# Input convolution as a projection, a copy and diagonal taps; split and softplus pieces placed elsewhere

## What is computed

```python
xz = einsum('btm,im->bti', x, W_in); x_d, z = split(xz, 2)      # 256 -> 2 x 512
xc = pad(x_d, 3 in front); xc = depthwise_conv(xc, conv_w)      # 4 taps along the tokens
x_d = silu(xc + conv_b)
dt, B, C = x_d @ W_x.T                                          # 1 + 16 + 16 columns
delta = softplus(dt * W_dt + b_dt)
for each token: h = exp(delta*A)*h + delta*B*x_d;  y = sum_s h*C      # 16 states
y = (y + D*x_d) * silu(z);  out = y @ W_out.T
```

## Time and profile before

| | us |
|---|---|
| median of 3 runs | 1176.44 |
| lowest, highest | 1171.94, 1177.12 |
| the profiled execution, its time | 1170.4 |
| its span, first to last instruction | 1168.6 |
| mixer, start of the gate of tile 0 to that of tile 9 | 99.15 to 742.48 |
| busy over the span: PE, DVE | 995.2 (85%), 958.2 (82%) |
| busy over the span: POOL, ACT | 792.6 (68%), 671.4 (57%) |

### The profile page before, as it was taken

How to read it: one execution, slowest core, us unless ns; L and a number is a source line. 1 busy time by engine, 2 the same in 40 slices (tenths; PEclk the granted TensorE clock), 3 DMA queues, 4 the chain that set the end, 5 groups by cost and what they waited for, 6 DMA issues and landing times.

```text
span 1168.6 us, 16964 instructions
## 1 busy us (share of the span) xinstructions
PE 995.2 (85%) x4739; PEld 757.7 (65%) x4739; DVE 958.2 (82%) x1813; ACT 671.4 (57%) x1780; POOL 792.6 (68%) x840
## 2 busy tenths in 40 slices
PE   6798889888798988989879797667599999999991
PEld 5686666666566665766656675334388888888780
...
GB/s 181 215 326 326 91 23 23 60 14 57 33 35 68 14 60 33 48 50 18 80 10 51 25 23 53 14 61 410 185 186 172 226 274 270 258 264 283 256 258 109
DMA packets 104475, 150.28 MB, mean 129 GB/s; under 512 B 13983, under 2 KB 91231, under 8 KB 103999
## 3 DMA queue, kind: packets, MB, share of 16 engines
...
HBM read 72.32 MB, written 76.82 MB: 128 GB/s over the span
## 4 chain that ended last, share of the span: by engine, by line
PE 47%; DVE 22%; issue 15%; ACT 8%; POOL 3%; DMA 3%; SPq 1%; DVEq 0%; POOLq 0%; ACTq 0%
PE BC L982 11%; PE Y L826 10%; DVE arena L1368 10%; PE F L747 5%; PE Y L976 3%; PE K L844 3%; PE K L996 3%; PE F L996 3%; DMA mixer_own<-pool_dram 2%; DVE arena L1380 2%; PE F L733 2%; PE D L988 1%; ACT arena L1038 1%; PE BC L808 1%; PE K L789 1%
## 5 line engine op out<-in xcount | busy, mean ns | idle before, releaser
L1368 DVE TENSOR_TENSOR_SCAN arena<-D,arena 128x444 f32<-128x444 f32 (+1 forms) x352 | 351.1, 1037 | 12.6 <-ACT D L1087 10.4
L826 PE MATMUL Y<-arena,ident 128*128 128x444 f32 (+1 forms) x704 | 308.4, 566 | 1.6 <-DVE arena L1380 1.6
L684 POOL DMA_INDIRECT gat<-y_dram,slot_all x176 | 175.6, 998 | 126.0 <-issue 105.5
L629 POOL TENSOR_TENSOR arena<-mixer_own,arena 128x888 f32<-128x888 f32 (+1 forms) x90 | 164.9, 1833 | 69.4 <-ACT arena L1075 64.8
L617 POOL DMA_INDIRECT pool_dram<-hrow,slot_of x176 | 175.7, 998 | 45.9 <-issue 38.6
L1087 ACT ACTIVATE D<-mixer_own,aneg 128x216 f32<-128x216 f32 (+1 forms) x384 | 148.2, 427 | 94.5 <-DVE arena L1368 91.8
L629 POOL TENSOR_TENSOR arena<-arena 128x888 f32<-128x888 f32 x75 | 143.6, 1915 | 69.1 <-ACT arena L1075 67.3
L1380 DVE TENSOR_TENSOR arena<-arena,BC 128x888 f32<-128x888 f32 (+1 forms) x176 | 184.9, 1050 | 5.7
L982 PE MATMUL BC<-arena,xt 128*128 x716 | 186.1, 383 | 0.0
L826 PEld LDWEIGHTS Y<-arena,ident 128*128 128x128 f32 x704 | 129.3, 203 | 75.2 <-issue 70.1
L1087 ACT ACTIVATE D<-arena,aneg 128x216 f32<-128x216 f32 x320 | 127.0, 437 | 83.0 <-DVE arena L1368 83.0
...
## 6 DMA issues: line engine op xcount, KB each, us to landing
mixer_own<-pool_dram SPq DMA_DIRECT2D x179, 144.0 KB, 3.7
y_dram<-mixer_own SPq DMA_DIRECT2D x179, 128.0 KB
...
```

Source lines behind the costliest of these rows:

```text
L629: nc.gpsimd.tensor_tensor(cut(drive[g % DRIVES], i), cut(du[i % 2], i), b_row[pooled(g) % B_ROWS][:, None, 0:width(i)].broadcast_to([P, KI ...
L684: nc.gpsimd.indirect_dma_start(out=gat[0:r, k, b, :], out_offset=None, in_=y_rows[0:(blocks_by(t) - k) * P, :], in_offset=bass.IndirectOff ...
L826: mm = nc.tensor.matmul(Y[j][:, 0:w], ident[:], read[g % 3][:, j * w:(j + 1) * w], start=(s == 0), stop=(s == STATES - 1), skip_group_chec ...
L1368: nc.vector.tensor_tensor_scan(state[g % 2][:, lo:hi], D[b][:, 0:hi - lo], drive[g % DRIVES][:, lo:hi], 0.0, ALU.mult, ALU.add).then_inc(s ...
```

## The change

The convolution is no longer folded into the weights. PE projects x (`project_x`: 2 groups x 2 matmuls, with the plain W_in), ACT copies the two groups to SBUF (`copy_x_d`, 128 x 444), and PE applies the 4 taps as 4 matmuls with diagonal 128 x 128 matrices (`diag_w`), and the bias as before. `project_x(n, 1)` stands in PE's step 4, c=2 and c=3 in steps 7 and 8, nothing of it in steps 5 and 6; `project_x` of the tile after next stands in step 14. The copies are in ACT's steps 4 and 14. DVE builds the 16 diagonals at the start instead of the 8 products of `inw4`, and the taps are loaded as 128 x 16 values in place of 128 copies of 2048.

Beside it: DVE's second split piece moves ahead of `reads` in step 12, `softplus_small` from step 12 to ahead of `reads` in step 13; POOL's `multiply_series` moves from step 13 to 14 and waits for `softplus_large`; ACT runs its split pieces ahead of the exp, the router's weights after the gate's tanh, copies B of state 15 early in step 12, and puts the logarithm before the series.

```diff
--- before.py
+++ after.py
@@ pool @@
             def multiply_series(n):
                 pool.wait_ge(series_done, n + 1)
+                pool.wait_ge(soft_sum, n + 1)
...
-                    if i + 1 < TILES and s == 13:
+                    if i + 1 < TILES and s == 14:
                         multiply_series(i + 1)
@@ pe @@
+            def project_x(n, b):
...
+                for c in range(2):
+                    for k in range(KM):
+                        at = 2 * b + c
+                        mm = nc.tensor.matmul(F[:, c * w:(c + 1) * w].rearrange("p (a t) -> p a t", t=TOKENS), inw_x[:, k, at * P:(at + 1) * P],
+                                              h0[n % 3][:, k, 0:images(n), :], start=(k == 0), stop=(k == KM - 1))
+                mm.then_inc(x_d_done, 1)
...
+            def convolve(n, c):
+
+                if c % 2 == 0:
+                    pe.wait_ge(x_d_copied, 2 * n + c // 2 + 1)
...
                 for back in range(TAPS):
-                    nc.tensor.matmul(to.rearrange("p (a t) -> p a t", t=TOKENS)[:, :, back:], inw4[:, k, TAPS - 1 - back, c * P:(c + 1) * P],
-                                     h0[n % 3][:, k, 0:images(n), 0:TOKENS - back], start=(k == 0 and back == 0), stop=False,
-                                     skip_group_check=True)
...
+                    nc.tensor.matmul(to.rearrange("p (a t) -> p a t", t=TOKENS)[:, :, back:], diag_w[:, c, TAPS - 1 - back, :],
+                                     of[:, :, 0:TOKENS - back], start=(back == 0), stop=False, skip_group_check=True)
...
-                if front and s in (4, 5):
-                    convolve(n, 2, s - 4)
+                if front and s == 4:
+                    project_x(n, 1)
...
-                if front and s in (6, 8):
-                    convolve(n, 3, (s - 6) // 2)
+                if front and s in (7, 8):
+                    convolve(n, s - 5)
...
-                    if s in (14, 15):
-                        convolve(i + 2, 0, s - 14)
+                    if s == 14:
+                        project_x(i + 2, 0)
+                    if s == 15:
+                        convolve(i + 2, 0)
@@ act @@
+            def copy_x_d(n, b):
+                act.wait_ge(x_d_done, 2 * n + b + 1)
+                if 2 * n + b > 0:
+                    act.wait_ge(conv_done, KI * n + 2 * b)
+                nc.scalar.activation(x_d[:, 0:2 * width(n)], F[:, 0:2 * width(n)], ACT.Copy).then_inc(x_d_copied, 1)
...
+                if front and s == 4:
+                    copy_x_d(n, 1)
+                if i + 2 < TILES and s == 14:
+                    copy_x_d(i + 2, 0)
...
                 if front and s == 11:
+                    split(n, 1)
                     softplus_exp(n)
-                    split(n, 1)
-                if back and s == 11:
-                    weights(t)
...
                 if front and s == 12:
                     nc.scalar.preload_act_table_set("natural_log_exp_and_others")
+                    if mix:
+                        copy_b(STATES * i + s + 3)
+                    softplus_ln(n)
                     softplus_series(n)
-                    softplus_ln(n)
@@ dve @@
+            def set_up_taps():
...
+                for c in range(KI):
+                    for a in range(TAPS):
+                        last = nc.vector.tensor_scalar(diag_w[:, c, a, :], ident[:], convw[:, c, a:a + 1], None, ALU.mult)
...
-                if front and s in (11, 12):
-                    split(n, s - 11)
-                if front and s == 12:
-                    softplus_small(n)
+                if front and s == 11:
+                    split(n, 0)
...
                         scan(g, 1)
+                    if i + 1 < TILES and s == 12:
+                        split(i + 1, 1)
+                    if i + 1 < TILES and s == 13:
+                        softplus_small(i + 1)
```

66 lines of the change are left out of this document (35 added, 31 removed).

## The result

The changed kernel takes 1146.5 us (median of 4 runs, 1145.88 to 1147.54); the kernel before took 1174.51 us on the same chip (4 runs, 1171.94 to 1177.12). The ratio is 0.9762, with an interval of 0.9734 to 0.979. The profiled executions have spans of 1145.2 and 1168.6 us.

The account below looks back on a forecast made before the run. DVE, busy 68.39 of 71.22 us a tile, was taken to bound the full tiles. Terms -20.7 (moved pieces), -6.5, +3.6 and -4 sum to -27.6 off the mean 1174.0: 1146 us, 8 in 10 between 1131 and 1163.

Parts of the forecast that it names:

- The split piece: DVE's step 12, piece moved ahead of `reads`: clear of POOL's product, 0.38 us instead of 2.07, 1.7 less a tile.
- softplus_large and the multiplication: DVE's `softplus_large` held by one POOL product only, 2.5 us for 3.29; the later `multiply_series` adds no wait at `softplus_sum`.
- both ways: Whether POOL's product or DVE's `softplus_large` comes first, tile 5 reaches 443.9 to 444.4 us in place of 446.13.
- The shared expert's wait: DVE's wait for ACT's tanh, 10.0 us in 8 tiles, goes; a later copy is held 0.4 more: net -6.5 us.
- ACT's copy: Step 4: ACT's copy waits for PE and delays the decays and a scan, 0.4 us a tile, +3.6 in all.
- PE: "Nothing": PE's convolution takes 3.2 us less a tile, worth nothing beyond what other terms count; step 7's added matmuls cost nothing.
- The third rival: ACT's step-4 copy, waiting for a late PE, becomes the bound, e.g. with PE at half clock: 1183 us; chance 0.05.
- Start and tile 0: Before the full tiles: less convolution on PE in the start, fewer held pieces in tile 0; together -4 us.
- the first: Rival: moved DVE pieces land in another POOL product, 1.5 us less gain a tile, 1160 us; chance 0.17.
- the second: Rival: everything is clear, no holds, multiplication and ACT's copy hidden: 19 us less, 1127; chance 0.2 for 1127 to 1137.
- The fourth: Rival: waits shift and POOL or PE take up DVE's gain; within 0.5% of 1176 us; chance 0.08.

Follow-up runs that it names:

- e9_product_13: Changed kernel with POOL's `multiply_series` alone back in step 13, ahead of that step's product, its new wait kept: 1271.58 us beside the changed kernel's 1269.39.

## Why the prediction was right, point by point

**The time** was forecast as 1146 and came out as 1146.5, within a sum that erred in three places. In the nine tiles the moved pieces gave 22.5 us where 20.7 were forecast, the convolution some 10 (1.1 a tile with the clock up) where 2.9 were, and the clock took back 10 where nothing was set down. That is 22, and the tiles measured 21.2, against 23.6 forecast. Ahead of the first gate and behind the tenth 2.2 us were gained, and not 4. Read between the profiled spans the gain is 23.4 us and not 27.6. The median fell by 28.0, because the profiled execution of before was among its kernel's shortest and that of after was not. The forecast took its 27.6 off the mean of all four times, and the sum's excess of 4 us over the profiled gain was met by a difference that no trace explains; that part of the agreement is luck.

**The split piece** was right: forecast 1.7 us a tile, 2.07 became 0.38. But it isn't worth that by itself, as its removal showed (621.6 against 622.2 us): the prediction added it to the next term, and the two depend on each other.

**softplus_large and the multiplication**: forecast 2.5 us, held once, with `softplus_sum` free of a wait for POOL. Measured 2.28, held once, by product 15 as said, and no such wait. The two terms together, forecast as 2.3 us, are 2.7 by the two durations and 2.5 between `glist` and gate. That "both ways" of the meeting with product 15 lead to the same was borne out only roughly: in `e9_product_13` DVE comes first and the stretch is 0.4 us shorter.

**The shared expert's wait** was forecast to go, and went. The copy L1494 takes 0.29 us where L1460 had 0.22; the 0.4 us more of hold that were set against the gain were 0.07.

**ACT's copy** was forecast at 0.4 us a tile. In a tile with the full clock it is 0.24, in one with the fall (from 372.76 us) 0.43; it lies in DVE's step 5 and not, as forecast, 6. With the two last terms the stretch from gate to `glist` was to be 0.4 us shorter, and is 1.1 shorter where the clock stays up.

**PE: "Nothing"** is the step that failed. The prediction counted PE's halved convolution as work off the path. It halved the work in step 0, PE fell idle behind the gate, and the clock went to half in seven tiles of nine: 1.5 us a tile, less the 0.4 that the same had cost before, 10 us in all. The third rival named the mechanism, half clock in the stretch ahead of the projection, and gave it 0.05 because the tile's mean clock was 0.98; a mean over 71 us could not show a fall of some 3 us, nor did it say that a lighter PE would bring one. Without the fall a tile takes 67.6 us and not the forecast 68.5; the mean of the nine, falls and all, is 69.1.

**Start and tile 0**: forecast -4, the first gate came 2.9 us earlier. Behind the tenth gate it is 0.7 us more. The first gate is not a firm figure, though: it comes at 97.0 to 101.1 us in the other runs with the old convolution, and at 95.4 to 100.4 in those with the new one. What moves it these runs don't show.

**The rivals.** No piece landed in a product that it was not expected to meet (the first). Everything clear, 1127 us (the second), is near what the changed kernel would have without the falls: 1146.5 less nine times 1.5 is some 1133, an estimate from the periods. The fourth, a time within 0.5% of 1176, is excluded by the result.
